# Storing eight tiles early and adding their last gated term by GpSimd's accumulating DMAs

## The reference

```
x = x + 0.5 * ffn(layernorm(x))
x = x + attention(layernorm(x))          # 32 heads, 8 key groups, width 128, causal, rotary
x = x + 0.5 * ffn(layernorm(x))          # the same weights as the first
```

```
def ffn(h):
    query = h @ Wq.T
    scores = (query @ Wr.T) @ (aux_keys @ Wr.T).T / sqrt(48) + log_rel     # 128 slots
    top 8 slots of each row; w = softmax(query . key / sqrt(64) + log_rel) over them
    aux = (w @ aux_values) @ Wvd.T @ Wvu.T
    u = clip(0.5 * log1p(var(h)) / mean(log1p(var(h))) + 2.5 * sigmoid(gelu(h @ Wu1.T + bu1) @ Wu2.T + bu2), 0, 5)
    gate = sigmoid(gate_w1 * clip((u - 0.5) / 1.5, 0, 1) + gate_bias);  0 where under 0.05
    return h + gate * aux
```

## Time and profile before

| | |
|---|---|
| time, median of 3 runs | 1425.04 us (1424.42 to 1427.04) |
| profiled execution, its time | 1426.41 us |
| its span, first to last instruction | 1423.6 us |
| busy: PE, DVE, ACT, POOL | 1351.8, 1177.8, 953.3, 704.9 us |
| DMA moved, mean rate | 211.20 MB, 148 GB/s |
| mean granted clock of TensorE | 0.984 |

### The profile page before, as it was taken

How to read it: one execution, slowest core, us unless ns; L and a number is a source line. 1 busy time by engine, 2 the same in 40 slices (tenths; PEclk the granted TensorE clock), 3 DMA queues, 4 the chain that set the end, 5 groups by cost and what they waited for, 6 DMA issues and landing times.

```text
span 1423.6 us, 25847 instructions
## 1 busy us (share of the span) xinstructions
PE 1351.8 (95%) x8474; PEld 754.3 (53%) x8604; DVE 1177.8 (83%) x2877; ACT 953.3 (67%) x2463; POOL 704.9 (50%) x596
## 2 busy tenths in 40 slices
PE   4779999998999999999999999999999999999995
PEld 3444555554455555555555555555555555555553
DVE  7887978889899887988878898889777798778657
ACT  5568777676677676667667667667666676666754
POOL 3376767677765344445545454435543454434321
PEclk8899999999999999999999999999999999999998
DMA  8466766787777566656567655657666677556443
GB/s 281 164 137 136 199 184 174 186 190 176 179 167 167 109 146 147 138 126 146 140 127 165 134 132 141 127 127 161 135 138 124 141 147 160 113 136 134 93 89 119
DMA packets 439828, 211.20 MB, mean 148 GB/s; under 512 B 382016, under 2 KB 383344, under 8 KB 439696
## 3 DMA queue, kind: packets, MB, share of 16 engines
q1 hardware_dynamic: 438144, 208.18, 63.6%
q10 hardware_dynamic: 1552, 1.38, 0.3%
HBM read 91.00 MB, written 25.17 MB: 82 GB/s over the span
## 4 chain that ended last, share of the span: by engine, by line
PE 70%; DVE 15%; ACT 5%; issue 4%; POOL 4%; DMA 1%; DVEq 0%; SPq 0%; ACTq 0%
PE PJ L1536 16%; PE PJ L1537 15%; PE PJ L1535 15%; DVE phl L1256 4%; PE PV L1708 4%; PE PV L1703 4%; PE PV L1704 4%; PE SC L1724 4%; PE SC L1722 4%; PE SC L1723 4%; POOL t L629 2%; ACT p L839 2%; DVE p L1246 2%; DVE t L1202 2%; DVE t L1200 1%
## 5 line engine op out<-in xcount | busy, mean ns | idle before, releaser
L651 POOL TENSOR_TENSOR oTl<-of,oTf 128x512 f16<-128x512 f32 x128 | 154.1, 1204 | 437.3 <-ACT oTf L831 437.1
L839 ACT ACTIVATE p<-p,mn 128x512 f32<-128x512 f32 (+3 forms) x512 | 280.9, 550 | 96.6 <-DVE mn L1246 96.5
L1256 DVE SCALAR_TENSOR_TENSOR phl<-p,ri,phl 128x128 f16<-128x128 f32 (+3 forms) x512 | 329.3, 683 | 0.0
L850 ACT ACTIVATE phl<-p,ri 128x128 f16<-128x128 f32 (+3 forms) x512 | 245.6, 550 | 4.1
L1535 PE MATMUL PJ<-XT,wsp 128*128 128x512 f16 x628 | 238.9, 380 | 4.0 <-DVE t L1202 3.9
L629 POOL TENSOR_TENSOR t<-t 128x512 f32<-128x512 f32 x158 | 201.7, 1277 | 77.3 <-DVE t L1202 76.8
L1536 PE MATMUL PJ<-XT,wsp 128*128 128x512 f16 x628 | 238.8, 380 | 0.0
L1537 PE MATMUL PJ<-XT,wsp 128*128 128x512 f16 x628 | 238.5, 380 | 0.0
L1246 DVE CUSTOM_DVE_ANT_0 p<-SC,maskw 128x512 f32<-128x512 f32 (+3 forms) x512 | 219.8, 485 | 2.1
L1536 PE MATMUL PJ<-wosp,oTf 128*128 128x512 f16 x512 | 194.0, 379 | 4.3
L634 POOL TENSOR_TENSOR qTl<-t,qTh 128x512 f16<-128x512 f32 x127 | 148.5, 1170 | 92.5 <-ACT qTh L815 92.5
(11 more groups left out here) (263 smaller groups left out, 2589.6 us busy)
## 6 DMA issues: line engine op xcount, KB each, us to landing
wsp<-kept SPq DMA_DIRECT2D x146, 256.0 KB, 3.0
wosp<-kept SPq DMA_DIRECT2D x96, 256.0 KB, 3.2
raw<-in_wqkv SPq DMA_DIRECT2D x48, 256.0 KB, 3.5
kept<-wsp SPq DMA_DIRECT2D x42, 256.0 KB, 2.5
raw<-in_wo SPq DMA_DIRECT2D x32, 256.0 KB, 4.4
kept<-wosp SPq DMA_DIRECT2D x32, 256.0 KB, 3.0
pTf<-phl SPq DMA_TRANSPOSE x256, 3.8
X<-in_x SPq DMA_DIRECT2D x3, 1024.0 KB, 9.8
```

The costliest lines, as they stand in the source:

```text
L839: ins = nc.scalar.activation(pt, pt, ACT.Exp, bias=mn[:, par, i:i + 1], scale=-1.0, accum_out=rs[:, par, i:i + 1])
L850: nc.scalar.activation(phl[:, par, high(i, 0):high(i, i) + 1:3, :], p[:, par, SOFF[i]:SOFF[i] + w].rearrange("p (k t) -> p k t", t=P), ACT ...
L1256: nc.vector.scalar_tensor_tensor(out=phl[:, par, low(i, 0):low(i, i) + 1, :], in0=p[:, par, SOFF[i]:SOFF[i] + w].rearrange("p (k t) -> p k ...
```

## The change

Eight tiles (0, 1, 2, 5, 6, 7, 8 and 9, all of the first three batches) are stored to the output when only their base is in X: SP issues three stores, of tiles 0 to 2 in step 50, 5 to 7 in step 82, 8 and 9 in step 114 (step 18 of batches 1, 2 and 3). In the tail ACT's `gated` writes the scaled auxiliary product of such a tile over the tile in X, and POOL issues a DMA that adds X's tile to the output in memory (`accum_op=ALU.add`). The other eight tiles (`BY_DVE`) are added by DVE and stored as before, in another order and cut: 3 and 4, 12, 13, 15, and 10 with 11 by SP, 14 by ACT. POOL's three additions are gone. The tasks of `TAIL` have other banks and another order, tile 11 last. `taken(n)` gives the semaphore that says that the bank of auxiliary n is consumed; `GATED` lists the tiles in TensorE's order. ACT makes the four base tiles of the last batch in one go, ahead of the gelu.

```diff
+STORE_AT = 18
...
-        + [(("AUX", 1, 1, n - 4), n) for n in (4, 5, 6)] + [(("ET", 1, 3, 0), 1)]
-        + [(("AUX", 1, n // 4, n % 4), k) for n, k in ((7, 7), (8, 3), (9, 0), (10, 2), (11, 4), (12, 5), (13, 6), (14, 7),
-                                                       (15, 3))])
+        + [(("AUX", 1, n // 4, n % 4), k) for n, k in ((4, 0), (5, 3), (6, 4))] + [(("ET", 1, 3, 0), 1)]
+        + [(("AUX", 1, n // 4, n % 4), k) for n, k in ((7, 5), (8, 2), (9, 7), (10, 6), (12, 0), (13, 1), (14, 3), (15, 4),
+                                                       (11, 5))])
+
+GATED = [4 * task[2] + task[3] for task, _ in TAIL if task[0] == "AUX"]
+BY_ACT = [0, 1, 2, 5, 6, 7, 8, 9]
+
+EARLY = [(0, 3), (5, 8), (8, 10)]
+BY_DVE = [3, 4, 12, 13, 14, 15, 10, 11]
...
@@ block.sync
                 for _, k, bb, i in side(SP_A, SP_B, s):
                     turn_normal(k, bb, i)
+                if s >= G * HG and s % (G * HG) == STORE_AT:
+                    c0, c1 = EARLY[s // (G * HG) - 1]
+                    sp.wait_ge(x_up[2], c1)
+                    sp.dma_start(out_v[:, c0:c1, :], X[:, c0:c1, :]).then_inc(st_out, 16)
             turn(NS - 1, 0)
             turn(NS - 1, 1)
-            for c0, c1 in ((0, 4), (4, 8), (8, 12), (12, 14), (15, 16)):
-                sp.wait_ge(r_xd[1], evens(c1))
-                sp.wait_ge(r_xp[1], c1 - evens(c1))
+            for c0, c1 in ((3, 5), (12, 13), (13, 14), (15, 16), (10, 12)):
+                sp.wait_ge(r_xd[1], BY_DVE.index(c1 - 1) + 1)
                 sp.dma_start(out_v[:, c0:c1, :], X[:, c0:c1, :]).then_inc(st_out, 16)
-            sp.wait_ge(st_out, 16 * 6)
+            sp.wait_ge(st_out, 16 * (len(EARLY) + 6))
+            sp.wait_ge(st_add, 16 * len(BY_ACT))
@@ block.gpsimd
-            def aux_add(n):
-                pool.wait_ge(x_up[2], n + 1)
-                pool.wait_ge(r_xa[1], n // 2 + 1)
-                nc.gpsimd.tensor_tensor(X[:, n, :], X[:, n, :], t1[:, n // 2 % NROPE, :], ALU.add).then_inc(r_xp[1], 1)
-
             out_lo(NS - 2)
             out_lo(NS - 1)
-            for n in odd:
-                aux_add(n)
+            pool.wait_ge(st_out, 16 * len(EARLY))
+            for n in BY_ACT:
+                pool.wait_ge(r_xa[1], BY_ACT.index(n) + 1)
+                pool.dma_start(out_v[:, n:n + 1, :], X[:, n:n + 1, :], accum_op=ALU.add).then_inc(st_add, 16)
@@ block.scalar
-            def aux_odd(n):
-                act.wait_ge(r_aux[1], n + 1)
-                act.wait_ge(r_gs[1], 1 if n < 12 else 2)
-                if n // 2 >= NROPE:
-                    act.wait_ge(r_xp[1], n // 2 - NROPE + 1)
-                nc.scalar.activation(t1[:, n // 2 % NROPE, :], bank(("AUX", 1, n // 4, n % 4)), ACT.Copy,
+            def gated(n):
+
+                act.wait_ge(r_aux[1], GATED.index(n) + 1)
+                act.wait_ge(r_gs[1], 1)
+                act.wait_ge(st_out, 16 * len(EARLY))
+                nc.scalar.activation(X[:, n, :], bank(("AUX", 1, n // 4, n % 4)), ACT.Copy,
                                      scale=gs[:, 1, n:n + 1]).then_inc(r_xa[1], 1)
...
-            for i in range(3):
+            for i in range(TB):
                 base(2, bb, i)
             gelu(1, bb, True)
             tail_sigmoid(9, 0, 12)
             exps_ffn(1, bb, (0, 1))
             exps_ffn(1, bb, (2,))
-            aux_odd(1)
-            aux_odd(3)
+            gated(0)
+            gated(1)
             exps_ffn(1, bb, (3,))
             tail_sigmoid(10, 12, NT)
+            gated(2)
             e_hi(1, bb)
-            aux_odd(5)
             tail_sigmoid(11, 12, NT)
-            base(2, bb, 3)
-            act.wait_ge(r_xd[1], evens(15))
+            for n in BY_ACT[3:]:
+                gated(n)
+            act.wait_ge(r_xd[1], BY_DVE.index(14) + 1)
             act.dma_start(out_v[:, 14:15, :], X[:, 14:15, :]).then_inc(st_out, 16)
@@ block.vector
             select(3)
-            add(0)
-            add(2)
             learned(1, bb)
             gate_1(1, 12, NT, 4)
             inverse_sums(1, 12, NT, 4)
-            add(4)
-            add(6)
+            add(3)
             dve.wait_ge(g_exd, 11)
             gate_2(1, 12, NT)
+            add(4)
             e_lo(1, bb)
-            add(7)
             dve.wait_ge(g_exd, 12)
             gate_3(12, NT)
             scales(1, 12, NT)
-            for n in range(8, NT):
+            for n in BY_DVE[2:]:
                 add(n)
```

More of the change, by code:

```diff
@@ L302, in macaron_kernel @@
                       "r_mn", "r_e", "r_t", "r_hi", "r_lo", "r_aux", "r_gs", "r_xd"))
-        r_xa, r_xp = {1: sem("r_xa1")}, {1: sem("r_xp1")}
+        r_xa, st_add = {1: sem("r_xa1")}, sem("st_add")
         g_ex, g_exd, g_act, a_z = sem("g_ex"), sem("g_exd"), sem("g_act"), sem("a_z")
@@ L356, in rope_index, with taken @@
             return 5 * n if kind == "K" else 5 * n + idx + 1
[L358 to L365, removed]
+        def taken(n):
+            return (r_xa[1], BY_ACT.index(n) + 1) if n in BY_ACT else (r_xd[1], BY_DVE.index(n) + 1)
         def consumed(task):
@@ L395, in consumed @@
             n = 4 * bb + i
-            if odd_tile(a, n):
-                return r_xa[a], n // 2 + 1
-            return r_xd[a], (evens(n) if a == 1 else n) + 1
+            return taken(n) if a == 1 else (r_xd[a], n + 1)
         def weight_slot(kind, n):
@@ L1182, in aux_add @@
                 n = 4 * bb + i
-                dve.wait_ge(r_aux[f], n + 1)
+                dve.wait_ge(r_aux[f], n + 1 if f == 0 else GATED.index(n) + 1)
                 dve.wait_ge(x_up[2 * f], n + 1)
```

## The result

| | before | after the change |
|---|---|---|
| time, median | 1425.04 us | 1433.78 us (1433.17 to 1435.13, 5 runs) |
| ratio, 95% interval | | 1.0059 [1.0048, 1.0070] |
| span of the profiled execution | 1423.6 us | 1432.5 us |

The change is slower by 8.7 us, 0.6%. The forecast was no change, and the range ended at 1428.6. The page, part 1 and part 3 (compare): the engines do what they did, and there is a new queue, q0, with POOL's descriptors, 1152 packets for eight DMAs.

A forecast was written before the change was run, and what follows sets the result against it. The prediction took the final stores on the DMA engines as the bound: starting 2.4 us earlier and losing a 3.1 us hole against 5.6 us of second reads, 0.1 us slower, rounded to nothing: 1425.0 us, range 1420.6 to 1428.6.

The forecast's parts named there:

- The sum: DMA engines in the tail: fed without a gap from 1405.7, 16.8 us of work to 1422.5, span end 1423.7.
- POOL's issue as the bound: Rival, tail: eight issues end to end from 1404.43; over 0.2% slower from 2.4 us each, 1430.3 us at 2.73; chance 0.07.
- my three signs: Signs of error: share under 1.0 with accumulations open; POOL issues end to end past 1415; span ending behind last plain store.
- The price of an accumulation: DMA engines in the tail: two passes, 1.40 us a tile against 0.70 for a plain store; chance 0.40.
- The cheap second read: Rival, tail: second read hides, 0.70 us a tile gives 1420.6 us, 1.0 us gives 1422.1; chance 0.33.
- the three passes: Rival, DMA engines in the tail: nothing overlaps, 2.10 us an accumulated tile, time 1430.7 us; chance 0.16.
- the slow rival: Same rival as the three passes; its reason: few 2 KB rows per engine, so latency covers badly; chance 0.16.
- The start of the flow: Tail: first accumulation's data starts at 1405.7, gated(0)'s end at 1404.43 plus 1.28 us for POOL's issue.
- POOL's hold on DVE: Tail: POOL's additions stretch a four-column DVE instruction (L1152, 0.88 us); removing them, 0.7 us on DVE, not counted as gain.
- Early stores: Steps 50, 82, 114: may hold the next transposes by up to 0.3, 0.9, 1.4 us; cost 0; rival, at most 2.6, chance 0.04.
- The engines' tail: TensorE, ACT, DVE: last DVE addition near 1413.5, or 1416 if TensorE's clock falls, against 1418.55; e_hi transposes start at 1405.5.
- What bounds the kernel: End of the kernel before: the stores, with DMA engines full (share 1.01) from 1414.0 to 1422.4 while compute engines run dry.

The follow-up runs named there:

- ring3k: The change with dynamic_dma_scratch_size 3072 instead of 1024 bytes a partition, nothing else; 1428.17 us, ratio to the kernel before 1.0017.
- 1280 bytes: The change with dynamic_dma_scratch_size 1280 instead of 1024 bytes a partition; one execution, 1427.94 us, span 1425.0 us.
- accs_only: ring3k without the tail's six plain stores and ACT's store of tile 14, so eight output tiles are never stored; one execution, 1423.36 us.
- no_acc: The change without POOL's eight accumulating DMAs, so eight tiles leave without their gated term; 1419.63 us, ratio to the kernel before 0.9962.
- pooladd: The change's order without early stores or POOL DMAs; POOL adds tiles 0 to 2, DVE the other thirteen, SP stores all; 1423.57 us, ratio 0.9989.
- plain_pool: The change with POOL's eight DMAs as plain stores without the addition; 1421.02 us, ratio to the kernel before 0.9968.

## Why the prediction was wrong, point by point

**The step that failed** is in "The sum": the five others "are issued from 1410.1 on, one each 1.28 us ... So the engines are fed without a gap". No issue came at 1410: POOL had no room for a fourth and stood until 1415.32. I costed an issue by its duration and had no term for what it needs in order to begin. The stops cost 5.6 us (the change against ring3k). The first stop is the longest and does little by itself: with 1280 bytes the only stop is one of 5.94 us, beside plain stores, and the time is ring3k's. The two behind it did the harm, because no plain store was left and tiles 8 and 9 each made a journey of its own, from 1423.7 to 1431.4. The nearest rival, POOL's issue as the bound, had the right engine and the wrong mechanism: an issue takes 1.06 us in the median (1.28 taken, 2.4 needed), and between the issues are 15.8 us, all but the first 0.9 of which POOL waits for landings. None of my three signs named this. The share fell to 0.00 when no accumulation was open, not "with accumulations open", and POOL's issues went on past 1415, but not end to end. With room for all eight (ring3k) the time is 2.6 us above the kernel before, just inside what I called no change; that rest belongs to the next two points.

**The price of an accumulation** was sized at 1.40 us, as two passes; it is 1.40 us only when many are queued, 1.51 us over eight (accs_only), 1.45 us beside stores (ring3k) and 2.0 us when one is alone. In ring3k that adds 0.4 us to the flow. Over eight it is 2.2 times a plain tile and 2.0 times when many are queued; the Trainium skill's ratio of 1.93 (Collectives: The Full Stack, section The bandwidth ceiling: the fold count and why AG ≠ RS ≠ AR) is a little under what the runs show. The cheap second read and the three passes are both out as prices; that an accumulation alone is slower than one in a queue is what the slow rival's reason, latency, would do, but no run tests that.

**The start of the flow** was set 1.28 us behind the end of gated(0). In the change gated(0) ends at 1405.2, the issue begins at 1405.86, takes 1.04 us, and the first bytes move in the window from 1407: 1.9 us. In ring3k too the flow starts at 1407.0, 1.3 us behind the forecast 1405.7; with the 0.4 us of the price its 17.2 us end at 1424.2 instead of 1422.5. Behind the flow pass 1.8 us there where 1.2 were forecast.

**POOL's hold on DVE**: I left the 0.7 us gain uncounted, "since an issue on POOL may hold DVE the same way". It hardly does; L1167 and L1169 beside an issue take 0.24 and 0.26 us (0.17 without), and L1156, the L1152 of before, takes 0.17 instead of 0.88. The gain was real and was of no use, because DVE no longer set the end.

**Early stores**, cost 0: right. The transposes' distance over step 50 is the same (9.05 us), and from there to the tail pass 791.5 us in the kernel before, 791.7 in the change, 791.6 in no_acc, and 791.3 in pooladd, which has no early store.

**The engines' tail**: right in its end. The last addition ends at 1415.08. TensorE's clock fell again: the window from 1405 to 1407 is granted 0.50, after 1408 it is 1.00. One wait was missed: auxiliary 5 starts only at 1404.35, when DVE has read the scores, so the transposes for e_hi start at 1406.89 behind auxiliary 6 and not behind ACT's last exponential.

**What bounds the kernel**: the DMA engines bound the kernel before, as I read it, and ring3k; in the change POOL's stops bound the end. plain_pool shows the engines' part from the other side: with eight plain second stores, and one short stop, it ends 4.5 us sooner than the kernel before.

## To carry to other kernels

A DMA from GpSimd needs room for its descriptors before it can be issued; count them against the program's scratch size (here three accumulations or seven plain stores of 128 x 512 in 1024 bytes). When the room is gone the engine stands until everything that it has issued has landed, so a burst of issues at the end of a kernel turns into round trips, here of 4 to 8 us. And moving work off the end by doing it in two halves pays only if the second half is cheaper than the whole: here a stored tile is 0.70 us and an added one 1.4 to 2.0 us on the DMA engines, which are the bound.

## What the runs showed of the hardware that I had not expected

POOL resumes 0.2 to 0.3 us after the last landing, and not after the first that would have made room: 1415.1 and 1415.32, 1423.4 and 1423.68, 1427.7 and 1427.91 in the change, 1415.4 and 1415.68 with 1280 bytes. The second of these is the plainest: by the count of 17 the fourth DMA's landing at 1420.9 would have made room for the seventh. The idle time is listed as "issue", with no releaser. An accumulation that has the engines to itself still keeps them at 1.02 for 2.0 us (the window from 1425 to 1427), longer than the 1.4 us of one in a queue. And a GpSimd DMA on 128 rows is issued in 0.54 us as a plain store and in 0.84 us or more with the addition.
